# The last 16 channels of a four-layer transformer's LayerNorm: scaled and shifted on GpSimd before the transpose, rounded and split on VectorE after it

## The chip, the cores and the metric

The program runs on one core of a Trainium2 chip. The metric is the device time of one execution in microseconds. The kernel before took 1564.3 us (median of 3 runs, 1563.18 to 1565.5).

## The reference

Four transformer layers run over 32 sequences of 128 tokens with 144 channels, in fp32. Each layer reads a condition vector and makes six rows per sequence from it: shift, scale and gate for attention, and the same for the MLP. What a layer does (layer 0; its MLP is a mixture of four experts, of which two are used per token):

```
mod = silu(c) @ w_adaln + b_adaln
sh_msa, sc_msa, g_msa, sh_mlp, sc_mlp, g_mlp = split(mod, 6)
h = layernorm(x) * (1 + sc_msa) + sh_msa
q, k, v = h @ w_qkv + b_qkv            # 16 heads of 9 channels
x = x + g_msa * (softmax(q k^T / 3) v @ w_proj + b_proj)
h = layernorm(x) * (1 + sc_mlp) + sh_mlp
x = x + g_mlp * mlp(h)                 # 144 -> 576 -> 144, gelu
```

Layers 1 to 3 have a plain MLP. Layer 2 uses an RMS norm in place of the LayerNorm, norms q and k by head, and passes its gates through tanh.

## The kernel before

**Blocks.** The 32 sequences are taken four at a time: a layer's attention has eight groups, its MLP eight steps. Each norm of four sequences is a block with a number k (16 per layer: eight for attention, eight for the MLP), 64 in all. `ORDER` lists the order in which the blocks are made and `NTH[k]` is a block's place in it.

**One block's norm.** The statistics come from VectorE (`stats`, L1443 and L1448), the factor from GpSimd (`factor`), and the normed rows `xn` (token by channel) from GpSimd (`rows`, L1923 and L1925) or in the MLP steps from VectorE (`normalise`). TensorE multiplies by channel, so `xn` is turned: its first 128 channels by `t_main` (L574), and ScalarE scales and shifts them by channel while it takes them out of PSUM (`mod_main`, L1166). The last 16 channels go a way of their own. GpSimd's `copies` (L1934) writes them four times side by side into `xr`, `t_rem` (L581) turns the 64 columns into 64 rows of a PSUM bank, and VectorE's `mod_rem` (L1471) scales and shifts them by channel into `hmod`, in four instructions, one for each sequence. ScalarE's `round_rem` (L1177) rounds `hmod` to `hhi` (fp32r), and VectorE's `split_rem` (L1477) writes `hr`, where two of the four copies carry the rounded value and two what it lacks. `hr` and `hT` are then the operands of every product of the block.

**The scales and shifts** for these 16 channels lie in `modr`, turned (channel by sequence). At the start, for each layer, TensorE computes `mod` (`layer_mods`), VectorE takes it out of PSUM (`mods_out`, L1847 and L1848), TensorE turns it (`turn_mods`) and VectorE takes it out again (`take_mods`, L1855 and L1856).

**Attention.** A group has eight units u, each for two head groups. In one unit TensorE makes scores for the maxima five units ahead (L648), VectorE takes the maxima (`head_max`, L1534), TensorE turns them (`turn_max`, L655, which waits for `d_on`), makes the scores again with the maxima taken off (L666, L670), ScalarE takes the exponential (L1223), TensorE weighs the values (L682) and turns the result (L690), and VectorE divides (`normed`, L1552, tile `On`). All engines run through lists written out by hand, in program order, and wait for semaphores alone. At u = 0 TensorE runs `t_rem` of the block three groups on, VectorE `mod_rem`; at u = 1 ScalarE rounds and VectorE splits, and TensorE waits for `d_hm` before it uses bank 5 again; at u = 4 and 5 VectorE takes the statistics of the next block, and GpSimd then makes its factor, its rows and its copies, in this order and after its other work of the group (`copy_rest`, `parts23`, `add_to_x`).

**DMAs.** q and k are written to DRAM and read back in another order (`write_parts`, L415 and L418, `read_parts`, L445, twelve DMAs for each block), all issued by SP in its own list. For each block SP also loads the gates, one row of DRAM to all 128 partitions (`load_gates`, L394). They were stored at the start by `save_gates` (L329). In the first group, SP's list is: write and read block 0's q and k, store the gates of the four layers, write and read block 1's, load the gates, load the rest of x and weights.

Of the kernel before, what the change touches and what calls it, by code (L numbers as in the profile page):

```python
# [7 lines left out]
F32 = mybir.dt.float32  # L8
# [11 lines left out]
L = 4  # L20
# [29 lines left out]
AHEAD = 5  # L50

# [47 lines left out]

def slot_of(k):  # L100
    l, which, g = k // 16, k % 16 // 8, k % 8
    if which == 0 and g < 3:
        return g if l == 0 else 2
    return g % 2


def build(nc, io):
    ctx = ExitStack()
    with ctx:
# [28 lines left out]
        modr = sb("modr", [REM - 2, L, 4, B])  # L138
# [7 lines left out]
        hmod = sb("hmod", [REM - 2, TG])  # L146
# [15 lines left out]
        ohi = hhi  # L162
# [30 lines left out]
        gsb = wfc2_f[0:2 * B, 0:L * C].rearrange("b (l n) -> b l n", l=L)  # L193
        vt = [wfc1[0:TOK_V[0], E - 1, 0:TG], wfc2[0:TOK_V[1], E - 1].rearrange("p k c -> p (k c)")[:, 0:TG]]
# [37 lines left out]
        cw_scr = nc.dram_tensor("cw_scr", [2, E, G, T], F32, kind="Internal").ap()  # L232
        gate_scr = nc.dram_tensor("gate_scr", [L, 2, B, C], F32, kind="Internal").ap()
# [31 lines left out]
        s_mod, d_ms = sem("s_mod"), sem("d_ms")  # L265

# [23 lines left out]
        def normal(k):  # L290

            return (d_xn, CR + 4 * (NTH_DVE[k] + 1)) if k in NTH_DVE else (g_xn, CR + 4 * (NTH_POOL[k] + 1))

# [14 lines left out]
        def _(sp):  # L308
# [157 lines left out]
            def attention(l):  # L466
                n0, m0 = 8 * l, 16 * l
                if l == 0:
                    write_parts(0, 0)
                    read_parts(0, 0)  # L470
                    for i in range(L):
                        save_gates(i)
                    write_parts(0, 1)
                    read_parts(0, 1)
                    sp.wait_ge(q_gs[0], 16)
# [4 lines left out]
                    for i in range(1, L):  # L480
                        sp.wait_ge(q_gs[i], 16)
                if l == 2:
                    write_parts(l, n0 + 1)
                    read_parts(l, n0 + 1)
                for g in range(8):
# [5 lines left out]
                    load_gates(m0 + g + 1)  # L491
                    if l == 0:
# [13 lines left out]
            def mlp(l):  # L506
# [8 lines left out]
                for g in range(8):  # L515
                    if g < 7 or l < 3:
                        load_gates(m0 + g + 1)
                    if l == 0 and g in (1, 2, 3):
# [23 lines left out]
        def _(pe):  # L542
# [16 lines left out]
            def turn_mods(l):  # L559
# [3 lines left out]
                for s in range(2):  # L563
                    pe.transpose(bank[4][:, 2 * B * s:2 * B * s + 2 * B], mods_m[:, s, :], ident[0:2 * B, 0:2 * B])
                for s in range(2):
# [181 lines left out]
            def attention(l):  # L747
# [39 lines left out]
                else:  # L787
                    pe.wait_ge(d_hm, CR + 4 * (NTH[m0 + 2] + 1))
                start_layer(l)
                for g in range(8):  # L790
                    n, m = n0 + g, m0 + g
                    new = turned_at(l, g)
                    for u in range(UNITS):
# [34 lines left out]
                        if u == 1 and g > 0:  # L828
                            if new is not None:
                                pe.wait_ge(d_hm, CR + 4 * (NTH[new] + 1))  # L830
# [32 lines left out]
                        elif u == 6 and g < 6:  # L863
# [4 lines left out]
                            else:  # L868
                                pe.wait_ge(d_hm, CR + 4 * (NTH[new] + 1))
                            values(l, n + 2, 1, 5)  # L870

            def values_unit(g, u, n, m, new):

                if u == 5 and g < 7:
# [4 lines left out]
                    else:  # L879
                        pe.wait_ge(d_hm, CR + 4 * (NTH[new] + 1))  # L880
# [8 lines left out]
            def by_token_unit(g, u, n, m, new):  # L889
# [16 lines left out]
                if u == 5 and g < 5:  # L906
                    if g:
                        pe.wait_ge(d_gate, CR + 2 * m)
                    else:
                        pe.wait_ge(d_hm, CR + 4 * (NTH[new] + 1))  # L910
# [14 lines left out]
            def mlp(l):  # L925
# [72 lines left out]
                def before(g):  # L998
# [4 lines left out]
                    if l < 3 and g in (4, 6):  # L1003
# [3 lines left out]
                        return (a_ht, CR + 4 * (NTH[k] + 1)), (d_hm, CR + 4 * (NTH[k] + 1))  # L1007
# [9 lines left out]
                    return (a_ht, CR + 4 * (NTH[m - 1] + 1) if m - 1 >= m0 else 0), (d_hm, CR + 4 * (NTH[m - 1] + 1))  # L1017

                def after_tile(g, t):
# [30 lines left out]
                    if l == 1 and g == 6 and t == 1:  # L1050
                        pe.wait_ge(d_hm, CR + 4 * (NTH[M + 1] + 1))
# [7 lines left out]
                def after_seq(g, b):  # L1059

                    first_of = turned_mlp(l, g)[0] if turned_mlp(l, g) else None
                    if l < 3 and g in (3, 5) and b == 1:
                        i = NTH[first_of]
                        turn(M + (g - 3) // 2, (a_ht, CR + 4 * (i + 1)), (d_hm, CR + 4 * (i + 1)))
                    if l == 1 and g in (4, 6):
                        n = N + (g - 4) // 2
                        o = 7 - b % 2
                        if b == 0:
                            pe.wait_ge(d_hm, CR + 4 * (NTH[first_of] + 1))
# [16 lines left out]
                    if l in (0, 2) and g in (4, 6) and b > 0:  # L1086
                        n = N + (g - 4) // 2
                        if b == 1:
                            pe.wait_ge(d_hm, CR + 4 * (NTH[first_of] + 1))
# [45 lines left out]
                if l == 1:  # L1135
                    pe.wait_ge(d_hm, CR + 4 * (NTH[M + 2] + 1))
# [17 lines left out]
        def _(act):  # L1154
# [15 lines left out]
            outs, rounds = [], []  # L1170

            def round_rem(k):
                act.wait_ge(d_hm, CR + 4 * (NTH[k] + 1))
                act.wait_ge(d_hr, CR + NTH[k])
                act.wait_ge(d_onr, CR + len(outs))
                rounds.append(k)
# [57 lines left out]
            def out_rem(n, o):  # L1234
                act.wait_ge(s_onr, CR + n + 1)
                act.wait_ge(d_onr, CR + n)
                act.wait_ge(d_hr, CR + len(rounds))
                outs.append(n)
                act.activation(ohi[:], bank[o][0:REM - 2, :], ACT.Copy).then_inc(a_oa, 1)

            def attention(l):
# [24 lines left out]
                for g in range(8):  # L1266
# [3 lines left out]
                    for u in range(UNITS):  # L1270
# [7 lines left out]
                        if u == 1 and new is not None:  # L1278
# [841 lines left out]
```

## Time and profile before

| | before |
|---|---|
| median of 3 runs | 1564.3 us |
| span of the profiled execution | 1547.8 us |
| TensorE busy | 1415.6 us, 91% |
| VectorE busy | 1036.5 us, 67% |
| ScalarE busy | 778.5 us, 50% |
| GpSimd busy | 542.2 us, 35% |
| mean granted TensorE clock | 0.969 |

The page gives the profiled execution's span, from its first to its last instruction, and no time of its own beside it. The median of the runs is 16.5 us above that span. Engines are named PE (TensorE), DVE (VectorE), ACT (ScalarE), POOL (GpSimd), SP; a busy share is an average over stages with different limits. An idle time in brackets behind an instruction names what ended it.

### The profile page before, as it was taken

What the parts mean: (1) busy time and instruction counts of PE and PEld (TensorE: products, weight loads), DVE (VectorE), ACT (ScalarE), POOL (GpSimd) and SP (SyncE); (2) the same over time, 40 slices, a digit from 0 to 9 for tenths busy, and PEclk for the clock granted to TensorE, in tenths of its full rate; (3) what the DMA queues carried; (4) which work ended last, traced back from release to release, by engine and by line L of the source; (5) the groups of instructions that cost most, each with busy time, mean ns of one, the idle gap of its engine ahead of it and who ended that gap; (6) DMA issues with size and microseconds to landing.
All of it is one profiled execution on the core that took longest, in us unless ns stands there. A gap on an engine that the chain in (4) does not pass through costs nothing. (4 is left out here: it accounts for less than half of the span.)

```text
span 1547.8 us, 41007 instructions
## 1 busy us (share of the span) xinstructions
PE 1415.6 (91%) x15976; PEld 1065.0 (69%) x15976; DVE 1036.5 (67%) x2592; ACT 778.5 (50%) x1287; POOL 542.2 (35%) x739
## 2 busy tenths in 40 slices
PE   5799988999999998999899778877999799999998
PEld 2377776777777776777676656766777577767776
DVE  4688885766676667888537689887446466666342
ACT  2377763333333335767645456665544266555543
POOL 3355532211131313555323423443335244343322
PEclk9799999999999999999999889999999899999999
DMA  4765631111122032565000333443116667775021
GB/s 129 149 163 147 161 88 52 51 44 44 35 58 75 19 94 62 144 150 138 20 31 22 104 95 104 109 115 104 33 36 86 114 102 109 138 138 97 24 55 47
DMA packets 209128, 134.92 MB, mean 87 GB/s; under 512 B 142461, under 2 KB 191320, under 8 KB 202730
## 3 DMA queue, kind: packets, MB, share of 16 engines
q1 hardware_dynamic: 188978, 129.74, 35.4%
q10 hardware_dynamic: 19960, 2.57, 1.2%
q8 instruction: 129, 2.11, 0.6%
q14 instruction: 61, 0.50, 0.1%
HBM read 98.24 MB, written 33.24 MB: 85 GB/s over the span
## 5 line engine op out<-in xcount | busy, mean ns | idle before, releaser
L1534 DVE TENSOR_REDUCE negm<-banks 128x8 bf16<-128x1024 f32 x256 | 311.1, 1215 | 79.0 <-PE banks L648 77.2
L1223 ACT ACTIVATE prob<-banks 128x1024 f32<-128x1024 f32 x256 | 262.3, 1025 | 194.0 <-PE banks L670 193.3
L1351 ACT ACTIVATE hid<-banks 128x512 f32<-128x512 f32 x144 | 85.9, 597 | 230.5 <-PE banks L951 230.5
L1954 POOL TENSOR_TENSOR X<-X,gx 128x288 f32<-128x288 f32 x128 | 104.7, 831 | 256.9 <-DVE gx L1564 255.1
L967 PEld LDWEIGHTS banks<-wfc,hid 128*128 128x128 f32 x1152 | 157.0, 190 | 30.0 <-issue 19.9
L666 PE MATMUL banks<-qk 54*128 54x128 bf16 (+1 forms) x2048 | 169.4, 236 | 5.7 <-ACT prob L1223 5.0
L670 PE MATMUL banks<-mT,identb 64*128 64x128 bf16 x2048 | 166.2, 225 | 0.3 <-issue 0.3
L967 PE MATMUL banks<-wfc,hid 128*128 128x144 f32 x1152 | 161.4, 286 | 0.0
L648 PE MATMUL banks<-qk 54*128 54x128 bf16 (+1 forms) x2048 | 123.3, 242 | 39.8 <-DVE negm L1534 24.9
L950 PE MATMUL banks<-hT,wfc 128*128 128x512 f32 x288 | 149.1, 599 | 1.7 <-DMA wfc<-in_L_cond_w 1.2
L1725 DVE TENSOR_TENSOR hid<-hid,qk 128x512 f32<-128x512 f32 x128 | 88.9, 695 | 88.8 <-ACT hid L1351 80.4
L682 PE MATMUL banks<-prob,V 128*32 128x128 f32 x4096 | 142.8, 281 | 0.0
L1471 DVE TENSOR_SCALAR hmod<-banks,modr 64x128 f32<-64x128 f32 x256 | 86.8, 396 | 77.4 <-PE banks L581 77.0
L1939 POOL CAST parts<-res 96x512 bf16<-96x512 f32 x96 | 58.5, 609 | 220.9 <-DVE res L1484 220.0
L1376 ACT ACTIVATE hid<-banks 128x512 f32<-128x512 f32 (+1 forms) x120 | 71.0, 595 | 122.1 <-PE banks L941 121.1
L987 PE MATMUL banks<-wfc,hid 128*128 128x144 f32 (+1 forms) x960 | 128.0, 290 | 0.2 <-DVE gx L1564 0.2
L648 PEld LDWEIGHTS banks<-qk 54*128 54x128 bf16 (+1 forms) x2048 | 70.2, 102 | 82.0 <-DVE negm L1534 38.1
L987 PEld LDWEIGHTS banks<-wfc,hid 128*128 128x128 f32 (+1 forms) x960 | 123.9, 194 | 3.9 <-issue 2.7
L940 PE MATMUL banks<-hT,wfc 128*128 128x512 f32 x240 | 123.5, 595 | 0.0
L682 PEld LDWEIGHTS banks<-prob,V 128*32 128x32 f32 x4096 | 106.7, 112 | 16.8 <-issue 6.4
L666 PEld LDWEIGHTS banks<-qk 54*128 54x128 bf16 (+1 forms) x2048 | 109.2, 101 | 9.6 <-ACT prob L1223 7.3
L1166 ACT ACTIVATE hT<-banks,modm 128x128 f32<-128x128 f32 x256 | 98.8, 453 | 33.2 <-PE banks L574 33.1
(165 smaller groups left out, 2799.2 us busy)
## 6 DMA issues: line engine op xcount, KB each, us to landing
qk<-qk_scr SPq DMA_DIRECT2D x96, 216.0 KB
gbuf<-gate_scr SPq DMA_DIRECT2D x64, 288.0 KB, 4.3
qk_scr<-parts SPq DMA_DIRECT2D x48, 288.0 KB, 2.7
qk<-qk_scr SPq DMA_DIRECT2D x96, 144.0 KB
qk<-cw_scr SPq DMA_DIRECT2D x8, 1024.0 KB, 4.7
qk_scr<-parts SPq DMA_DIRECT2D x48, 144.0 KB, 2.5
qk<-qk_scr SPq DMA_DIRECT2D x96, 72.0 KB
qk<-tok_scr SPq DMA_DIRECT2D x32, 216.0 KB
```

Source lines behind the costliest of these rows:

```text
L648: mm = pe.matmul(bank[s][:, T * i:T * i + T], operand(l, 0, n, U, s, i), operand(l, 1, n, U, s, i), start=True, stop=True)
L666: pe.matmul(bank[2 + s][:, at], operand(l, 1, n, U, s, i), operand(l, 0, n, U, s, i), start=True, stop=False)
L670: mm = pe.matmul(bank[2 + s][:, at], one_hot(half, 64 * s + 4 * (u % 2) + i, [64, T]), mT[half, u // 2, :], start=False, stop=True)
L682: mm = pe.matmul(bank[4][32 * i:32 * i + 32, T * (2 * s + u % 2):T * (2 * s + u % 2 + 1)], V[:, n % 3, u // 2, VS * h:VS * h + 32], prob[: ...
L940: pe.matmul(bank[2 + i % 2][:], wfc1_t[:, at:at + 128], hT[:, h, :], start=True, stop=False)
L950: pe.matmul(bank[2 + i % 2][:], w, hT[:, h, :], start=True, stop=False)
L967: mm = pe.matmul(bank[4 + b // 2][:, C * (b % 2):C * (b % 2) + C], hid[:, i % KT, T * b:T * b + T], wfc2[:, e - (t == KT - 1), t, :], star ...
L987: mm = pe.matmul(bank[4 + q][:, C * (b % 2):C * (b % 2) + C], hid[0:rows, t, T * b:T * b + T], wfc2[0:rows, k, t, :], start=(t == 0), stop ...
L1166: act.activation(hT[:, slot_of(k), T * b:T * b + T], bank[o][:, T * b:T * b + T], ACT.Identity, scale=modm[:, l, 2 * w + 1, at:at + 1], bi ...
L1223: act.activation(prob[:, 2 * (U % 3):2 * (U % 3) + 2, :], pairs[1][:], ACT.Exp, scale=scale).then_inc(a_exp, 1)
L1534: dve.tensor_reduce(negm[:, u // 2, :, 4 * (u % 2):4 * (u % 2) + 4], pairs[0][:].rearrange("q s (h k) -> q s h k", k=T), AX.X, ALU.max, ne ...
L1954: pool.tensor_tensor(x, x, gx[:, q, :, :], ALU.add).then_inc(g_x, 1)
```

## The change

The last 16 channels are scaled and shifted by token, before they are turned. The condition rows of these channels (shift, and one plus scale) are written by VectorE to `msr` and stored by SP to a new DRAM tensor `mod_scr`, one store for each layer (`save_mods`), each right behind that layer's gate store. For each block from the fourth on (`FIRST = 3`), SP loads the block's rows, 128 numbers, to all 128 partitions, into one of four buffers `mrow` (`load_mods`). GpSimd's `copies` multiplies the 16 channels in place and adds the shift while it writes them four times. After the transpose VectorE rounds (`tensor_copy`) and splits in two instructions that both read the PSUM bank (`round_and_split`), both at the place of `mod_rem`; `split_rem` at unit 1 and ScalarE's `round_rem` are gone. TensorE's waits for `d_hm` become waits for `d_hr` (`rem_taken`). The first three blocks keep the old way. `modr` holds layer 0 alone; for the other layers the transposes of its rows and their copies are left out. `hmod` and `modr` lie in other tiles' room, and `ohi` has room of its own, so ScalarE's `out_rem` no longer waits for the split of a norm.

```diff
+            def save_mods(l):
+                sp.wait_ge(d_ms, CR + l + 1)
+                sp.dma_start(mod_scr[l].rearrange("w b s c -> (w b) s c"), msr[:, l]).then_inc(q_ms[l], 16)
+
+            def load_mods(k):
+                i, l, w, g = NTH[k], k // 16, k % 16 // 8, k % 8
+                sp.wait_ge(q_ms[l], 16)
+                if i >= FIRST + NMR:
+                    sp.wait_ge(g_xr, CR + i - NMR + 1)
+                sp.dma_start(mrow[:, i % NMR].rearrange("t b s c -> t (b s c)"),
+                             mod_scr[l, w, G * g:G * g + G].rearrange("b s c -> (b s c)").unsqueeze(0)
+                             .to_broadcast([T, G * 2 * CR_CH])).then_inc(q_mr[i % NMR], 16)
...
                     for i in range(L):
                         save_gates(i)
+                        save_mods(i)
                     write_parts(0, 1)
                     read_parts(0, 1)
+                    load_mods(3)
+                    for k in prepared_in(0, 0, 0):
+                        load_mods(k)
                     sp.wait_ge(q_gs[0], 16)
                     load_gates(0)
...
                     load_gates(m0 + g + 1)
+                    for k in prepared_next(l, 0, g):
+                        load_mods(k)
...
+            def round_and_split(k, o):
+                dve.wait_ge(s_hr, CR + NTH[k] + 1)
+                dve.wait_ge(d_hr, CR + NTH[k])
+                dve.tensor_copy(hhi[:], bank[o][0:REM - 2, :]).then_inc(d_hi, 1)
+                dve.wait_ge(d_hi, CR + NTH[k] - FIRST + 1)
+                dve.scalar_tensor_tensor(hr[0:REM - 2, slot_of(k), :], hhi[:].bitcast(F32), masks[0:REM - 2, 0:1],
+                                         bank[o][0:REM - 2, :], ALU.mult, ALU.add).then_inc(d_hr, 1)
...
                         if u == 0 and new is not None:
-                            mod_rem(new, 5)
-                        if u == 1 and new is not None:
-                            split_rem(new)
+                            round_and_split(new, 5)
...
-                pool.tensor_copy(xr[:, p], xn[:, p, :, CM:C].unsqueeze(2).to_broadcast([T, G, 4, CR_CH])).then_inc(g_xr, 1)
+                if k < FIRST:
+                    pool.tensor_copy(xr[:, p], xn[:, p, :, CM:C].unsqueeze(2).to_broadcast([T, G, 4, CR_CH])) \
+                        .then_inc(g_xr, 1)
+                    return
+                pool.wait_ge(q_mr[i % NMR], 16 * ((i - FIRST) // NMR + 1))
+                x, by = xn[:, p, :, CM:C], mrow[:, i % NMR]
+                pool.tensor_tensor(x, x, by[:, :, 1, :], ALU.mult).then_inc(g_ml, 1)
+                pool.wait_ge(g_ml, CR + i - FIRST + 1)
+                pool.tensor_tensor(xr[:, p], x.unsqueeze(2).to_broadcast([T, G, 4, CR_CH]),
+                                   by[:, :, 0, :].unsqueeze(2).to_broadcast([T, G, 4, CR_CH]), ALU.add).then_inc(g_xr, 1)
```

## Rows read from the trace of the kernel before

**Rows 1.** The page's busy times: us, share of the span, instructions.

```profile
PE 1415.6 (91%) x15976; PEld 1065.0 (69%) x15976; DVE 1036.5 (67%) x2592; ACT 778.5 (50%) x1287; POOL 542.2 (35%) x739
```

**Rows 2.** TensorE's waits: line, releaser: us in total, times, longest.

```profile
PE banks L655 <- DVE On L1552: 33.2, 42, 1.6
...
PE banks L648 <- DMA qk<-qk_scr: 9.9, 7, 2.8
PE banks L581 <- POOL xr L1934: 8.3, 12, 1.8
```

**Rows 3.** Stretches: length; PE, PEld, DVE, ACT, POOL busy (count); clock; DMA share; GB/s.

```profile
65.00:242.00 177.00, 164.55 (x2973) 126.48 (x2977) 147.99 (x332) 120.97 (x174) 88.00 (x110) 0.97 0.55 136
...
900.00:1108.00 208.00, 170.45 (x3048) 137.60 (x3050) 175.25 (x419) 130.99 (x214) 80.78 (x131) 0.96 0.36 94
```

**Rows 4.** Tiles `hmod`, `hhi`: ns min/median/max; one wait: us, times.

```profile
L1471 DVE TENSOR_SCALAR hmod<-banks,modr x256: 390/394/404, 19.5 to 1529.2; 64x128 f32<-64x128 f32 x128
...
L1477 DVE SCALAR_TENSOR_TENSOR hr<-hhi,masks,hmod x64: 739/744/1225, 22.4 to 1530.3; 64x512 fp32r<-64x512 f32 x64
  ACT hhi L1177: 43.7, 59
...
L1558 DVE SCALAR_TENSOR_TENSOR onr<-hhi,masks,banks x32: 728/734/742, 97.8 to 1460.5; 64x512 fp32r<-64x512 f32 x32
```

**Rows 5.** GpSimd by line: ns min/median/max, first and last start.

```profile
L1934 POOL COPY xr<-xn x39: 396/396/852, 89.1 to 1094.4; 128x256 f32<-128x256 f32 x39
...
L1903 POOL TENSOR_TENSOR rstd<-mv x16: 195/198/214, 800.0 to 1187.3; 128x4 f32<-128x4 f32 x16
...
L1954 POOL TENSOR_TENSOR X<-X,gx x128: 779/795/1259, 102.2 to 1544.1; 128x288 f32<-128x288 f32 x128
```

**Rows 6.** Order of time, layer 0, groups 3, 4: start, us, what, [idle before].

```profile
148.49 1.22 DVE L1534 TENSOR_REDUCE negm<-banks 128x8 bf16<-128x1024 f32 x1 [0.32 <-PE banks L648]
...
158.50 0.40 POOL L1934 COPY xr<-xn 128x256 f32<-128x256 f32 x1
...
159.04 0.60 PE L581 MATMUL banks<-ident,xr 128*64 128x128 f32 x4 [0.26 <-POOL xr L1934]
```

**Rows 7.** Order of time: the first and the last of 17 hand-overs.

```profile
89.14 0.41 POOL L1934 COPY xr<-xn 128x256 f32<-128x256 f32 x1
...
89.70 0.38 PE L581 MATMUL banks<-ident,xr 128*64 128x128 f32 x2
...
1068.43 0.40 POOL L1934 COPY xr<-xn 128x256 f32<-128x256 f32 x1
...
1068.97 0.49 PE L581 MATMUL banks<-ident,xr 128*64 128x128 f32 x3 [1.36 <-POOL xr L1934]
```

**Rows 8.** Order of time, TensorE, layer 2, group 3, unit 3.

```profile
992.96 0.23 PE L655 MATMUL banks<-identb,negm 128*128 128x128 bf16 x1 [1.59 <-DVE On L1552]
...
994.17 0.40 PE L648 MATMUL banks<-qk 54*128 54x128 bf16 x8 [0.98 <-DMA qk<-qk_scr]
```

**Rows 9.** The start: SP's reads; DMA landings of L394 (all; 59:61), L329; TensorE; clock.

```profile
55.69 4.24 SPq L445 DMA_DIRECT2D qk<-qk_scr  x12
...
DMA to landing us min/median/max: 3.0/4.3/14.1
...
DMA to landing us min/median/max: 14.1/14.1/14.1
...
DMA to landing us min/median/max: 1.8/7.9/10.1
...
66.98 1.06 PE L581 MATMUL banks<-ident,xr 128*64 128x128 f32 x4
...
54.00:67.00 13.00, 6.05 (x83) 3.87 (x83) 7.61 (x8) 2.31 (x2) 3.40 (x5) 0.50 0.69 134
```

**Rows 10.** Layer 3: SP's waits from 1325 to 1395 us; TensorE at 1390.

```profile
SPq L450 <- DMA v_scr<-wfc: 18.1, 3, 6.9
...
1390.94 0.64 PE L648 MATMUL banks<-qk 62*128 62x128 bf16 x8 [2.16 <-DMA qk<-tok_scr]
```

More of the change, by code:

```diff
@@ L50 @@
 AHEAD = 5
+FIRST = 3
+NMR = 4
 def norm_order():
@@ L97, with prepared_in, prepared_next @@
 NTH_DVE = {k: i for i, k in enumerate(BY_DVE)}
+def prepared_in(l, w, g):
+    if w:
+        return prepared_mlp(l, g)
+    return [turned_at(l, g + 1)] if g < 6 else [16 * l + 8 + g - 4]
+def prepared_next(l, w, g):
+    l, w, g = l + (w and g == 7), (w + (g == 7)) % 2, (g + 1) % 8
+    return prepared_in(l, w, g) if l < L else []
 def slot_of(k):
@@ L137, in build @@
         modm = sb("modm", [CM, L, 4, B])
-        modr = sb("modr", [REM - 2, L, 4, B])
+        mrow = sb("mrow", [T, NMR, G, 2, CR_CH])
         gbuf = sb("gbuf", [T, 2, G, C])
@@ L232, in build @@
         cw_scr = nc.dram_tensor("cw_scr", [2, E, G, T], F32, kind="Internal").ap()
+        mod_scr = nc.dram_tensor("mod_scr", [L, 2, B, 2, CR_CH], F32, kind="Internal").ap()
         gate_scr = nc.dram_tensor("gate_scr", [L, 2, B, C], F32, kind="Internal").ap()
@@ L265, in build @@
         s_mod, d_ms = sem("s_mod"), sem("d_ms")
+        q_ms, q_mr = [sem(f"q_ms{l}") for l in range(L)], [sem(f"q_mr{i}") for i in range(NMR)]
+        g_ml, d_hi = sem("g_ml"), sem("d_hi")
         block = ctx.enter_context(nc.Block())
@@ L517, in mlp @@
                         load_gates(m0 + g + 1)
+                    for k in prepared_next(l, 1, g):
+                        load_mods(k)
                     if l == 0 and g in (1, 2, 3):
@@ L563, in turn_mods @@
                 for s in range(2):
-                    pe.transpose(bank[4][:, 2 * B * s:2 * B * s + 2 * B], mods_m[:, s, :], ident[0:2 * B, 0:2 * B])
-                for s in range(2):
+                    mm = pe.transpose(bank[4][:, 2 * B * s:2 * B * s + 2 * B], mods_m[:, s, :], ident[0:2 * B, 0:2 * B])
+                for s in range(2 if l == 0 else 0):
                     mm = pe.transpose(bank[4][0:REM - 2, 2 * B * (s + 2):2 * B * (s + 3)],
@@ L829, in attention @@
                             if new is not None:
-                                pe.wait_ge(d_hm, CR + 4 * (NTH[new] + 1))
+                                pe.wait_ge(*rem_taken(new))
                             else:
@@ L868, in attention @@
                             else:
-                                pe.wait_ge(d_hm, CR + 4 * (NTH[new] + 1))
+                                pe.wait_ge(*rem_taken(new))
                             values(l, n + 2, 1, 5)
@@ L879, in values_unit @@
                     else:
-                        pe.wait_ge(d_hm, CR + 4 * (NTH[new] + 1))
+                        pe.wait_ge(*rem_taken(new))
                     values(3, n + 1, 1, 5)
@@ L909, in by_token_unit @@
                     else:
-                        pe.wait_ge(d_hm, CR + 4 * (NTH[new] + 1))
+                        pe.wait_ge(*rem_taken(new))
                     q_and_k_by_token(n + 3, 0, 5)
@@ L1847, in mods_out @@
                 dve.tensor_copy(mods_m, src[:, :, 0:CM])
-                dve.tensor_copy(mods_r, src[:, :, CM:C].unsqueeze(2).to_broadcast([2 * B, 2, 4, CR_CH])).then_inc(d_ms, 1)
+                if l == 0:
+                    dve.tensor_copy(mods_r, src[:, :, CM:C].unsqueeze(2).to_broadcast([2 * B, 2, 4, CR_CH]))
+                dve.tensor_copy(msr[:, l, 0], src[:, 0, CM:C])
+                dve.tensor_scalar(msr[:, l, 1], src[:, 1, CM:C], 1.0, None, ALU.add).then_inc(d_ms, 1)
             def take_mods(l):
                 dve.wait_ge(s_mod, CR + l + 1)
-                for out, src in ((modm[:, l], bank[4][:, 0:4 * B]), (modr[:, l], bank[4][0:REM - 2, 4 * B:8 * B])):
+                both = ((modm[:, l], bank[4][:, 0:4 * B]), (modr[:], bank[4][0:REM - 2, 4 * B:8 * B]))
+                for out, src in both if l == 0 else both[:1]:
                     out = out.rearrange("c (w s) b -> c w s b", s=2)
```

48 lines of the change are left out of this document (20 added, 28 removed).

## The prediction

> **What bounds the kernel now.** I read the page first, then TensorE's waits, the busy times by stage, the tiles that the change touches, and last the order of time around each hand-over. TensorE is busy 91% of the span and VectorE 67% [rows 1]. What frees VectorE is therefore worth something only where TensorE waits for it. The list of TensorE's waits is short: 33.2 us for `On` ahead of the transpose of the maxima (L655), and 8.3 us in 12 waits for GpSimd's `xr` (L581) [rows 2]. The `On` waits lie mostly in layer 2's attention: there VectorE is busy 175.25 of 208 us and TensorE 170.45, while in layer 0's attention TensorE has 164.55 of 177 us [rows 3]. So VectorE is near its limit in one stage of four, and the path that starts each group's LayerNorm transpose (statistics on VectorE, then GpSimd, then L581) is tight elsewhere.
>
> **What the change removes.** For 61 of the 64 blocks, VectorE's four scale-and-shift instructions go (394 ns each by the median), and ScalarE's rounding, for which VectorE stood idle 43.7 us in 59 waits before its split (744 ns) [rows 4]. What comes in their place is one copy out of PSUM and one split that reads PSUM. The split has a twin: the attention output's one, 734 ns [rows 4]. The copy (64x512 to SBUF) has no row of its own shape; it lies between one of the 394 ns pieces (a quarter of it) and the 734 ns of the two-operand form. I take 0.65 us. So at unit 0 of a group VectorE does 0.65 + 0.05 for its own semaphore + 0.73 = 1.4 us, where it did 4 x 394 = 1.6 us with overlaps (1.36 from first to last), and in unit 1 some 0.65 us of split and up to 0.6 us of waiting go. VectorE gains about 1.3 us a group, TensorE sees bank 5 released at the same time within 0.1 us. ScalarE's 61 roundings are off the path: none of TensorE's listed waits names them; I cost them at nothing.
>
> **What it is worth in layers 0, 1 and 3: nothing.** In layer 0's group 3 (groups and units count from 0), before the statistics that start GpSimd, VectorE already stands idle for TensorE's scores (0.32 us at 148.49) [rows 6]. A VectorE that reaches that point earlier waits longer, and the statistics at unit 5 come when they came.
>
> **What it is worth in layer 2's attention.** There TensorE waits 1.59 us for `On` at unit 3, and right behind that 0.98 us for a q/k read [rows 8]. With the split gone from unit 1, `On` is 0.66 us earlier (0.744 less the overlap). In the groups where the q/k read lands last (of TensorE's seven such waits, 9.9 us in all [rows 2], one each in groups 2, 3, 4 and 6) this is handed to the DMA. Groups 0, 1 and 5 keep it: 3 x 0.66 = 2.0 us. Against it stand 0.3 us for the new semaphore step ahead of TensorE's unit 1. I take -1.7 (0 to -4: all six groups keep it).
>
> **What it adds on GpSimd.** `copies` was one COPY of 256 elements a partition, 396 ns. Now it is a product over 64 elements, a semaphore, and a sum over 256 written with repeats. GpSimd's two-operand rows are 198 ns at 4 elements and 795 ns at 288 [rows 5], so 2.1 ns an element: 0.20 + 60 x 2.1 ns = 0.33, and 0.20 + 252 x 2.1 ns = 0.72. With 0.08 between (the spacing of dependent steps of GpSimd) that is 1.13, less 0.40: **0.73 us more**. Ends: 0.28 (the sum as cheap as the copy, the product at the 198 ns floor) and 1.3 (both at the 0.795 of 288 elements).
> Is it hidden? At 158.50 GpSimd starts the copy, 0.40 us, and L581 starts at 159.04, 0.14 us after its end, having waited 0.26 us [rows 6]. The same 0.14 to 0.15 us separates the two in 17 attention groups (six of layer 0, six of layer 1, five of layer 2; the first and the last in [rows 7]) and in two steps of layer 1's MLP. In these the copy's end is what releases TensorE or comes with it, so each lengthens by 0.73, unless another wait follows that was already longer:
> - layer 0: five groups pay, the sixth loses it to a 1.6 us wait for q/k, another of the seven: 5 x 0.73 = 3.65;
> - layer 1: five pay and the sixth in part (0.3): 3.95;
> - layer 1's MLP: 2 x 0.73 = 1.5;
> - layer 2: covered by the `On` wait at unit 1 and the q/k waits: 0. If that cover goes, 3.6.
> In layer 3 the copy stands over 4 us ahead of its reader: 0.
>
> **What it adds on SP's queue, at the start.** Block 3's copies now wait for `mrow`, whose load SP issues behind the twelve q/k reads of the second block. Those reads start at 55.69 and take SP 4.24 us; the gate load issued right behind them, at 60.03, lands 14.1 us later, at 74.1, where the median of its kind takes 4.3 us [rows 9]. The load of block 3 takes its place ahead of the gates. Lower end: the small gate stores issued behind the first block's reads waited up to 10.1 us [rows 9], which is 14.3 us after that block's first read (35.4), so 55.9 + 14.3 = 70.2 here (the four new stores cost SP about one issue, 0.4 us, the shorter set-up gives back 0.2). Upper end: 74.3. I take the middle, 72.3. Then 1.13 for the pair and 0.15 to TensorE: L581 at 73.6 instead of 66.98 [rows 9], **+6.6** (4.5 to 8.6). GpSimd's copy was done at 57.5 before, so this cover of 9.5 us is eaten whole. TensorE stands idle meanwhile behind L581, with q/k of block 2 and the next scores queued after it. The 0.7 us wait for a q/k read in group 1, the shortest but one of the seven, goes: -0.7. The clock: from 54 to 67 us it was granted 0.50, the lower level of 1.2 GHz, with TensorE busy 6.05 of 13 us [rows 9]; after a longer idle time work that ran at 2.4 GHz will run at the lower level a while: +1.0 (0 to 3). Sum of the start: **+6.9**.
> The set-up also loses two small transposes and two small VectorE instructions for each of three layers, about 0.5 us, which now only lengthens the wait.
>
> **What it adds on SP's queue later.** One more issue for each block (0.34 us, as the gate load) and 64 KB in 512-byte rows. In layers 0 to 2 it follows the group's reads, and the next writes are far off: 0. In layer 3 SP is itself late: between 1325 and 1395 us it waits for no `parts` at all, only for `v_scr` (18.1 us in 3 waits) and its own writes, and TensorE waits 2.16 us for q/k at 1390.94 [rows 10]. Each turn of that loop gets 0.4 us of issue and up to as much of transfer; four turns before the wait at 1390.94, at 0.5 each: **+2.0** (0 to 4).
>
> **Sum**: start 6.9, layer 0 3.65, layer 1 3.95, its MLP 1.5, layer 2 -1.7, layer 3 2.0: +16.3. The profiled execution's span is 1547.8 us and becomes 1564.1. The median of the runs, 1564.3, is 16.5 us above that span; I carry this over unchanged: 1564.3 + 16.3 = **1580.6 us**, 1.0% slower.
>
> **The rivals.**
> 1. *The load overtakes the reads.* If `mrow` lands some 3 us after its issue at 60.4, block 3 is ready at 64.7, ahead of 66.98, and the start costs 0 in place of 6.9: 1573.7. For it: the four `gate_scr` stores had a minimum of 1.8 us; against it: that one was issued after the reads were through, and the gate load took 14.1 us. 12%.
> The Trainium skill, "DMA: Bandwidth & Descriptors", section "Queues, rings and completion order", says that completion is not in order of issue, since one DMA may use fewer of the 16 engines than another; by it a small load on free engines could overtake. The gate load of the same 128-row form did not [rows 9].
> 2. *GpSimd's pair is cheap* (0.28 us): the 12.4 paying hand-overs cost 3.5 and not 9.1: 1575. 14%.
> 3. *Faster: VectorE's queue is the bound of the attention groups of layers 0 to 2.* It is busy 148 of 177 and 175 of 208 us [rows 3]. If each of 18 groups became shorter by the 1.3 us that VectorE saves, and GpSimd's delay went under it, -23.4 + 6.9 = -16.5: 1548. It decides from the point where the statistics of unit 5 come earlier than before. Against it: VectorE's idle time for scores just ahead of them [rows 6] and `xr` as TensorE's own wait. 9%.
> 4. *Heavier*: the pair costs 1.3 us, layer 2's cover gives way, and layer 3's loop takes 1 us a turn: 16.3 + 12.4 x 0.57 + 3 + 2 = +28.4: 1592.7. 12%.
> 5. A mixture near zero (rivals 1 and 2 together with all of layer 2's gain): 6.9 + 5.6 + 2.3 = 14.8 less of 16.3, so 1566: 5%.
> The forecast keeps 48%. Range for 8 in 10: 1568 to 1590, which leaves out rivals 3 to 5 for the most part. A measurement of this kernel tells about 0.2%, 3 us, from no change: slower 0.86, same 0.05, faster 0.09.
>
> **What would show it.** In the changed kernel's trace: L581 of block 3 (about 67 us before) starts at 72 to 75 us behind a wait of 5 us or more for GpSimd; GpSimd's pair takes 1.0 to 1.3 us; the waits of L581 for `xr` rise from 8.3 to some 22 us; layer 3's waits for `tok_scr` reads rise from 2.8 to near 5 us; VectorE's busy time falls by 50 us or more without shortening layers 0 and 1. I am wrong if layer 0's or layer 1's groups become shorter, or if block 3 starts on time.

## The result, and the profile after

The changed kernel takes 1581.43 us (median of 4 runs, 1572.6 to 1584.25); the kernel before took 1563.74 us beside it (4 runs, 1560.69 to 1565.5). The ratio is 1.0096 with a 95% interval of [1.0062, 1.013]: slower by 15 us (the two medians are 17.7 us apart). The forecast was 1580.6 us. The total is right, and the experiments below show that one of its terms was well off. Ratios, here and below, leave out runs more than 1.5% above the fastest of their kernel: 3 of 93 of the kernel before, and 2 of one other kernel.

The page of the changed kernel, its span and busy times (as [rows 1]):

```profile
span 1570.8 us, 40884 instructions
...
PE 1423.7 (91%) x15970; PEld 1072.7 (68%) x15970; DVE 1001.3 (64%) x2408; ACT 748.5 (48%) x1226; POOL 582.7 (37%) x800
```

VectorE lost 35 us of work, ScalarE 30, and GpSimd got 40.5 more. For VectorE 50 or more were predicted. That comes out (55) with the four scale-and-shift instructions at their full length of 394 ns each; they overlap, and with the 1.36 us from first to last that the prediction names itself it is 42. In layer 0's group 3 VectorE's busy time fell by 0.73 us (20.94 to 20.21, rows under the experiments), which makes 44 us for 61 blocks; the rest of the difference to 35 was not looked into. TensorE's waits in the changed kernel (as [rows 2]: line, releaser, us in total, times, longest; L627 is the old L581, L694 the old L648, L701 the old L655):

```profile
PE banks L627 <- POOL xr L1984: 26.5, 20, 6.9
...
PE banks L701 <- DVE On L1595: 23.9, 39, 1.8
PE banks L694 <- DMA qk<-qk_scr: 9.3, 6, 3.5
PE banks L694 <- DMA qk<-tok_scr: 9.1, 5, 2.9
```

Waits for `xr` rose from 8.3 to 26.5 us (predicted: some 22), those for `On` fell from 33.2 to 23.9.

**The start**, in order of time: SP's issue of block 3's load, GpSimd's pair, TensorE's transpose (as [rows 9]):

```profile
59.98 0.82 SPq L364 DMA_DIRECT2D mrow<-mod_scr  x2
...
73.52 0.32 POOL L1982 TENSOR_TENSOR xn<-xn,mrow 128x64 f32<-128x64 f32 x1 [15.76 <-DMA mrow<-mod_scr]
73.92 0.72 POOL L1984 TENSOR_TENSOR xr<-xn,mrow 128x256 f32<-128x256 f32 x1
...
74.70 0.64 PE L627 MATMUL banks<-ident,xr 128*64 128x128 f32 x2 [6.89 <-POOL xr L1984]
```

The load lands 13.4 us after its issue, at 73.4 (predicted 72.3), and L627 starts at 74.70 (predicted 73.6) behind 6.89 us of idle time. The landing, from the answer for that line:

```profile
DMA to landing us min/median/max: 13.4/13.4/13.4
```

The stretches around it (columns as in [rows 3]):

```profile
54.00:67.00 13.00, 5.53 (x74) 3.32 (x75) 7.60 (x8) 2.72 (x3) 3.65 (x5) 0.50 0.76 165
67.00:74.00 7.00, 0.80 (x16) 0.54 (x12) 0.00 (x0) 1.02 (x1) 0.40 (x2) 0.50 1.00 155
74.00:90.00 16.00, 14.20 (x192) 8.91 (x194) 9.71 (x17) 8.38 (x13) 5.93 (x7) 0.82 0.36 109
```

TensorE is idle for 6.2 of the 7 us from 67, and in the 16 us behind them the clock is granted at 0.82, a mixture of its two levels. Before, the transpose ran at 66.98 [rows 9]. Group 0 of layer 0 as a whole (from its first exponential to the next group's), before and changed:

```profile
64.93:87.23 22.30, 20.09 (x329) 14.11 (x333) 15.92 (x36) 14.55 (x22) 8.24 (x11) 0.87 0.74 158
```

```profile
65.69:95.52 29.83, 20.74 (x329) 14.57 (x333) 15.27 (x33) 14.04 (x20) 9.28 (x13) 0.76 0.56 123
```

It grew by 7.5 us, 6.9 of them the wait.

**The pair** on GpSimd in all 61 blocks (ns min/median/max, first and last start), and VectorE's two instructions:

```profile
L1982 POOL TENSOR_TENSOR xn<-xn,mrow x61: 317/319/382, 73.5 to 1534.0; 128x64 f32<-128x64 f32 x61
L1984 POOL TENSOR_TENSOR xr<-xn,mrow x61: 718/723/1121, 73.9 to 1534.4; 128x256 f32<-128x256 f32 x61
```

```profile
L1518 DVE CAST hhi<-banks x61: 673/682/684, 75.8 to 1551.3; 64x512 fp32r<-64x512 f32 x61
L1520 DVE SCALAR_TENSOR_TENSOR hr<-hhi,masks,banks x61: 737/740/740, 76.5 to 1552.0; 64x512 fp32r<-64x512 f32 x61
```

0.32 and 0.72 us stand against a predicted 0.33 and 0.72; 0.68 and 0.74 against 0.65 and 0.73.

**A hand-over of layer 0** (as [rows 6]), and the next one:

```profile
169.56 0.72 POOL L1984 TENSOR_TENSOR xr<-xn,mrow 128x256 f32<-128x256 f32 x1
...
170.42 0.38 PE L627 MATMUL banks<-ident,xr 128*64 128x128 f32 x2 [0.99 <-POOL xr L1984]
...
193.70 0.38 PE L627 MATMUL banks<-ident,xr 128*64 128x128 f32 x2 [1.00 <-POOL xr L1984]
```

The idle time was 0.26 us [rows 6] and is 0.99 now. From this hand-over to the next it is 193.70 - 170.42 = 23.28 us; before, the next one came at 181.58, 22.54 us on. That is 0.74 more in this group, as forecast (0.73):

```profile
181.58 0.60 PE L581 MATMUL banks<-ident,xr 128*64 128x128 f32 x4 [0.26 <-POOL xr L1934]
```

By stage, without the start: layer 0's groups 1 to 5 went from 114.2 to 118.1 us (+3.9, predicted 3.65), layer 1's attention from 171.9 to 175.1 (+3.2, predicted 3.95), its MLP from 135.8 to 138.8 (+3.0, predicted 1.5), layer 2's attention from 207.7 to 209.2 (+1.5, predicted -1.7), layer 3's from 218.8 to 224.4 (+5.6, predicted 2). Two traces can't settle such totals, and that the first two are near the forecast is in part luck. Layer 0's five groups changed by 0.0, +1.6, +0.7, +0.7 and +0.7 us: in group 1 the pair's 0.7 stands against a read wait of 0.65 us that did not come back, in group 2 another 0.9 us is not the pair's. In layer 1 the groups 3 and 4, for which 0.73 each were forecast, changed by 0.0 and +0.1, and group 5 grew by 1.7, of which 1.25 are an idle time of TensorE with no releaser in the profile. In the last three stages the changed kernel's trace has more time at the clock's lower level (3.7 us more in layer 1's MLP, 10 in layer 2's attention, 5.3 in layer 3's; 3.2 in layer 1's attention too), and such time comes and goes between executions of one kernel, as the next section shows.

### The profile page after: what moved, and what is told of

The parts are those of the page before. It is cut to its first block and busy times, and to the rows that moved or that the text cites. A ratio compares the mean times of both kernels' runs of the same rounds, so it can differ in the third digit from the quotient of the medians.

```text
span 1570.8 us, 40884 instructions
## 1 busy us (share of the span) xinstructions
PE 1423.7 (91%) x15970; PEld 1072.7 (68%) x15970; DVE 1001.3 (64%) x2408; ACT 748.5 (48%) x1226; POOL 582.7 (37%) x800
## 5 line engine op out<-in xcount | busy, mean ns | idle before, releaser
L694 PE MATMUL banks<-qk 54*128 54x128 bf16 (+1 forms) x2048 | 123.4, 242 | 46.0 <-DVE negm L1577 24.2
L728 PE MATMUL banks<-prob,V 128*32 128x128 f32 x4096 | 147.4, 287 | 0.0
L694 PEld LDWEIGHTS banks<-qk 54*128 54x128 bf16 (+1 forms) x2048 | 70.2, 102 | 89.0 <-issue 42.3
L728 PEld LDWEIGHTS banks<-prob,V 128*32 128x32 f32 x4096 | 109.9, 114 | 17.7 <-issue 7.2
L1992 POOL TENSOR_TENSOR parts<-res,parts 96x512 bf16<-96x512 f32 x96 | 112.7, 1174 | 7.7
```

What stands on the lines that cost most here:

```text
L694: mm = pe.matmul(bank[s][:, T * i:T * i + T], operand(l, 0, n, U, s, i), operand(l, 1, n, U, s, i), start=True, stop=True)
L728: mm = pe.matmul(bank[4][32 * i:32 * i + 32, T * (2 * s + u % 2):T * (2 * s + u % 2 + 1)], V[:, n % 3, u // 2, VS * h:VS * h + 32], prob[: ...
L1992: pool.tensor_tensor(parts[:, m, 2, :], res[:, i % 2, :], parts[:, m, 1, :], ALU.subtract).then_inc(g_p3, 1)
```

## What one trace can and can't tell here

The kernel before was profiled a second time, unchanged, in one run. What was on record:

> The kernel before, profiled once more, to see what of its first profile repeats. Theory (the first profile, 1547.8 us, was an execution with little time at the lower clock): span near 1560 us, time at the lower clock near 120 us in place of 94; the busy and idle pattern of layers 0 to 2 the same to 0.1 us outside stretches at the lower clock; tok_scr waits in layer 3 anywhere from 2 to 9 us. Rival (the profile is typical and the timed runs carry 16.5 us outside the span): span within 3 us of 1547.8.

Measured: 1572.84 us. Spans and mean granted clocks of the first and the second trace of the same kernel:

```profile
core 0: 1547.8 us, clock 0.969
```

```profile
core 0: 1571.0 us, clock 0.957
```

The second is 23.2 us longer. Its waits for `On` and `xr` are the same as in [rows 2]. Its waits for reads are longer: 12.0 us for `qk_scr` where the first had 9.9, and 6.0 us in 3 waits for `tok_scr` in layer 3 where the first had 2.8. So what I had expected of layers 0 to 2, the same pattern to 0.1 us, holds for the engines' own waits and not for the reads (layer 0's group 1 waits 1.41 us for one, 0.65 in the first trace):

```profile
PE banks L655 <- DVE On L1552: 33.1, 42, 1.6
PE banks L648 <- DMA qk<-qk_scr: 12.0, 8, 3.1
...
PE banks L648 <- DMA qk<-tok_scr: 6.0, 3, 3.0
```

Most of what grew is the same work in stretches at the lower level. Layer 1's group 4, first trace and second (columns as in [rows 3]):

```profile
681.88:704.89 23.01, 21.95 (x393) 16.70 (x396) 19.79 (x42) 16.25 (x24) 12.50 (x17) 1.00 0.61 152
```

```profile
692.40:719.16 26.76, 23.51 (x393) 17.80 (x395) 19.77 (x42) 16.27 (x24) 12.48 (x17) 0.94 0.52 126
```

The same 393 matmuls take 23.01 and 26.76 us; the clock is the difference in the row (1.00 and 0.94), with 1.56 of the 3.75 us in TensorE's busy time. The other 2.2 us are idle time: TensorE's longest wait in this group is 2.56 us with no releaser in the profile (0.36 in the first trace). What it waited for is not shown. In the 93 runs of the kernel before that stand beside my experiments, the time reaches from 1551.6 to 1585.0 us and the mean granted clock from 0.971 to 0.952; time at the lower level (the granted clock is 1.00 or 0.50, so it is twice what the mean lacks of 1, times the span) reaches from 90 to 152 us, and it correlates with the time at 0.85.

This corrects one step of the forecast. The "16.5 us" between the span and the median are nothing that lies around a span: in every run on record, of every kernel here, time less span is 1.8 to 1.9 us. [Rows 1] come from an execution with little time at the lower level, faster than the median one. The prediction carried the 16.5 us over from before to after, which did no harm: it makes the forecast the median before plus 16.3.

## The experiments

Each ratio is against the kernel before, timed in between on the same chip, with its 95% interval. The first kernels build the change up from its parts.

**VectorE's half alone.** GpSimd copies as before, VectorE has the new two instructions, and there is no store, load or wait for them. The kernel leaves out the scale and shift of the 16 channels from the fourth block on. Against the changed kernel (`save_mods`, `load_mods` and SP's waits for `q_ms` are out at all their places):

```diff
-                        save_mods(i)
...
-                    load_mods(3)
-                    for k in prepared_in(0, 0, 0):
-                        load_mods(k)
...
-                pool.wait_ge(q_mr[i % NMR], 16 * ((i - FIRST) // NMR + 1))
-                x, by = xn[:, p, :, CM:C], mrow[:, i % NMR]
-                pool.tensor_tensor(x, x, by[:, :, 1, :], ALU.mult).then_inc(g_ml, 1)
-                pool.wait_ge(g_ml, CR + i - FIRST + 1)
-                pool.tensor_tensor(xr[:, p], x.unsqueeze(2).to_broadcast([T, G, 4, CR_CH]),
-                                   by[:, :, 0, :].unsqueeze(2).to_broadcast([T, G, 4, CR_CH]), ALU.add).then_inc(g_xr, 1)
+                pool.tensor_copy(xr[:, p], xn[:, p, :, CM:C].unsqueeze(2).to_broadcast([T, G, 4, CR_CH])).then_inc(g_xr, 1)
```

> The changed kernel with GpSimd's single COPY of 256 elements as before, without the stores and loads of the condition rows and without the wait for them. Left out of the computation: scale and shift of the last 16 channels from the fourth block on. What stays is VectorE's and ScalarE's half of the change. My theory (only layer 2's attention waits for VectorE): layer 0 and 1 groups last as before (22.2 to 23.4 us), layer 2's attention gains 1 to 4 us, the whole is 0 to 5 us faster than before: ratio to before 0.997 to 1.000. Rival (VectorE's queue bounds the attention groups of layers 0 to 2): 18 groups shorter by 1.3 us each, 23 us faster, ratio 0.985.

Measured: 1554.36 us, ratio 0.9931 [0.9903, 0.996]. TensorE's waits:

```profile
PE banks L692 <- DVE On L1586: 26.4, 41, 1.4
...
PE banks L685 <- DMA qk<-tok_scr: 7.7, 5, 4.0
```

The half that I had priced at -1.7 us (0 to -4) gives -10.8 by its ratio. Layer 3's reads are to be seen as well: 7.7 us of waits for `tok_scr` in a kernel that loads nothing new.

**The same once more**, on another chip, with no edit:

> VectorE's half alone once more, beside the two kernels with part of the loads on the same chip: ratio 0.993 as before if its gain of 10 us is real, where my prediction allowed 0 to 4. Left out: as above. If it comes out above 0.997, the gain was a draw of the clock and the prediction's small figure stands.

Measured: 1555.45 us, 0.9946 [0.9914, 0.9977]. The mean of the two is 0.9938, 9.6 us. The gain stands, though this interval reaches up to -3.6 us, just inside my 0 to -4.

**With the stores and loads, unread.** The first kernel plus SP's four stores and 61 loads, for which nobody waits; it leaves out the same scale and shift. Against the changed kernel only GpSimd's part of the diff above is left: the wait and the pair go, the copy comes.

> As the kernel with VectorE's half alone, plus the four stores and the 61 loads, which nothing waits for and nothing reads. Left out of the computation: the same scale and shift. My theory (SP's list and the DMAs cost time in layer 3's attention alone): layer 3's attention longer by 3 to 6 us than in the kernel without loads, with TensorE's waits for tok_scr reads rising from under 3 us to 7 to 10 us; layers 0 to 2 and the start within 1 us. Rival (layer 3's longer waits come from the later phase against the clock or from VectorE's half): no difference between the two kernels.

Measured: 1559.13 us, 0.9977 [0.9949, 1.0005]: 4.8 us over the kernel without them by the medians, 7 by the ratios.

**With the wait.** GpSimd waits for `mrow` ahead of its copy, and still only copies. Against the kernel with the unread loads:

```diff
+                pool.wait_ge(q_mr[i % NMR], 16 * ((i - FIRST) // NMR + 1))
```

> As the one before, with GpSimd's wait for the loads kept, and the single COPY in place of product and sum. Left out of the computation: the same scale and shift. My theory: the first group pays for the load of block 3 alone, 6 to 7 us more than without the wait (L581's counterpart starts at about 74 us behind a wait of 6 us), and nothing else moves. Against the changed kernel it shows the price of the pair: 0.65 us for each of some 12 to 13 hand-overs, so 8 to 10 us faster than the changed kernel. Rival (the pair is hidden but for the first group): within 2 us of the changed kernel.

Measured: 1565.55 us, 1.0007 [0.998, 1.0035]: +6.4 us by the medians, +4.7 by the ratios. The first copy behind the wait starts at 75.1 us, so it is this wait and no other (GpSimd stands idle for it for 16.2 us, once). In its trace group 0 of layer 0 takes 29.95 us, where the kernel without the wait has 21.74:

```profile
L1981 POOL COPY xr<-xn x61: 397/398/477, 75.1 to 1532.1; 128x256 f32<-128x256 f32 x61
```

**The loads ahead of the reads.** The complete change, but the loads of blocks 3 and 4 are issued between the writes and the reads of block 1's q and k:

```diff
                     write_parts(0, 1)
-                    read_parts(0, 1)
                     load_mods(3)
                     for k in prepared_in(0, 0, 0):
                         load_mods(k)
+                    read_parts(0, 1)
```

> The changed kernel, complete, with the loads for blocks 3 and 4 issued before the twelve q/k reads of block 1 in SP's list and not behind them. My theory (the load stands in the queue behind the reads): it lands within 3 to 4 us of its issue at 53 us, block 3's transpose starts at 66 to 68 us without a wait, and the kernel is 6 to 9 us faster than the changed one. Rival (the load is slow by itself, or the first group waits for something else next, as the clock): gain under 3 us.

Measured: 1568.75 us, 1.0025 [0.9996, 1.0053], 11 us less than the change by the ratios. The issue, and the landing of the first loads:

```profile
53.35 1.50 SPq L364 DMA_DIRECT2D mrow<-mod_scr  x2
```

```profile
DMA to landing us min/median/max: 4.1/4.3/4.4
```

GpSimd's sum is done at 59.45 us. TensorE's transpose waits for GpSimd no longer, and the clock rises in the stretch in which the changed kernel stood idle:

```profile
68.20 1.06 PE L627 MATMUL banks<-ident,xr 128*64 128x128 f32 x4
```

```profile
67.00:74.00 7.00, 6.76 (x83) 4.09 (x83) 3.46 (x5) 3.42 (x5) 1.27 (x2) 0.73 0.94 166
```

So the wait at the start has one cause, the load's place behind the twelve reads: the same load lands in 4.1 to 4.4 us ahead of them and in 13.4 us behind them. The Trainium skill, "DMA: Bandwidth & Descriptors", section "Why a DMA increments its semaphore by 16 and not by 1", says that a DMA runs on up to 16 engines that finish independently, and that only the full count means that all data landed. By that a load is as late as the latest of its parts. The landings of 13.4 and 4.3 us are in keeping with it; which engines held it back no run here shows.

This kernel is also the second way to the pair's price. It differs from the kernel with the unread loads by the pair, GpSimd's wait (which costs nothing here) and the order of the loads. It is 7.5 us slower by the ratios and 9.6 by the medians, on the same chip.

The next kernels start from this order and take the remaining costs one by one.

**Layer 3's loads earlier.** In layer 3's attention, the loads of groups 0 to 5 are issued ahead of `turn_values`:

```diff
                         if l == 3:
+                            for k in prepared_next(l, 0, g):
+                                load_mods(k)
                             turn_values(n0 + g + 2)
                     load_gates(m0 + g + 1)
-                    for k in prepared_next(l, 0, g):
+                    for k in prepared_next(l, 0, g) if l < 3 or g > 5 else []:
```

> The kernel with the early loads, and in layer 3's attention each block's load issued right behind the q/k reads, ahead of SP's wait for v_scr, and not between that wait and the next writes. Theory A (each load lengthens layer 3's loop of writes, reads and v_scr by its issue and its bytes): the issue leaves the loop, gain of 1 to 3 us over the kernel with the early loads, tok_scr waits near 4 us. Theory B (the tok_scr waits vary from run to run and do not come from the loads, since the kernel without any load had 7.7 us of them): no difference beyond 1 us.

Measured: 1564.05 us, 1.0008 [0.9986, 1.0029], which doesn't part from 1.0025. The wait that it was aimed at, for `tok_scr`, did not shrink: 9.0 us in 5 waits, where the kernel with the early loads has 6.6 in 3.

**The last 16 channels first.** GpSimd norms these channels of a block, makes the pair, and only then norms the first 128, in the attention blocks of layers 0, 1 and 3 (`part` is `rows` for a range of channels):

```diff
                 factor(k)
-                rows(k)
-                copies(k)
+                if k < FIRST or k // 16 == 2:
+                    rows(k)
+                    copies(k)
+                    return
+                part(k, slice(CM, C), g_xm)
+                copies(k, g_xm)
+                part(k, slice(0, CM), g_xn)
```

> The kernel with the early loads, and on GpSimd, in the attention of layers 0, 1 and 3, the last 16 channels normed first (4 x 64-partition-wide small instructions of 128x16), then the pair, and the 128 channels for the main transpose after it. Theory (GpSimd's chain from the statistics to xr releases TensorE in the groups of layers 0 and 1): xr is ready some 2.3 us earlier (3.4 us of rows become 1.1), TensorE's waits of L627 in layers 0 and 1 (0.6 to 1.8 us in each of 12 groups) go to zero, groups last 22.2 to 22.5 us, and the kernel is 8 to 14 us faster than the one with the early loads, 5 to 9 us faster than before. Rival (the groups are bound by something just behind, VectorE's On or the q/k reads): gain under 4 us.

Measured: 1560.03 us, 0.9965 [0.9943, 0.9988]. It beats both the change and, by 0.35%, the kernel before. GpSimd's order in one group, and TensorE's transpose, which starts without a wait:

```profile
153.79 2.16 POOL L1946 TENSOR_SCALAR xn<-X,mv,rstd 128x16 f32<-128x16 f32 x4
...
156.03 0.32 POOL L1999 TENSOR_TENSOR xn<-xn,mrow 128x64 f32<-128x64 f32 x1
156.43 0.73 POOL L2001 TENSOR_TENSOR xr<-xn,mrow 128x256 f32<-128x256 f32 x1
157.13 3.19 POOL L1946 TENSOR_SCALAR xn<-X,mv,rstd 128x128 f32<-128x128 f32 x4
...
157.64 0.60 PE L628 MATMUL banks<-ident,xr 128*64 128x128 f32 x4
```

Layer 0's group 3 took 23.44 us before and 24.18 in the changed kernel, and takes 22.76 here (group 4: 22.55, 23.27 and 22.13):

```profile
132.93:156.37 23.44, 21.75 (x393) 16.65 (x396) 20.94 (x44) 16.25 (x24) 13.51 (x17) 1.00 0.56 146
```

```profile
142.84:167.02 24.18, 21.75 (x393) 16.65 (x396) 20.21 (x41) 15.82 (x23) 14.09 (x18) 1.00 0.53 141
```

```profile
132.64:155.40 22.76, 21.82 (x393) 16.70 (x395) 20.06 (x41) 15.82 (x24) 15.77 (x22) 1.00 0.59 156
```

All three rows are at the clock's full level, so this comparison is clean of it.

**Both** (the two diffs together):

> Both of the above on top of the early loads. If the two are independent, the sum of their gains: 9 to 16 us faster than the kernel with the early loads.

Measured: 1559.14 us, 0.996 [0.9934, 0.9987]. Against the kernel with layer 3's loads earlier alone, beside it on the same chip, the order of the channels is worth 4.9 us by the medians, 7.5 by the ratios. Layer 3's edit again shows nothing of its own.

**Which loads cost.** VectorE's half again, with the loads of layers 0 to 2 alone and with layer 3's alone, unread:

```diff
             def load_mods(k):
+                if not (l < 3):      # the other kernel: l == 3
+                    return
```

> VectorE's half with the stores and the loads for the blocks of layers 0 to 2 alone (45 of 61; nothing waits for them). Left out of the computation: scale and shift of the last 16 channels from the fourth block on, as in VectorE's half. Theory A (the loads cost time only in layer 3's loop of writes and reads): as VectorE's half alone, ratio to before 0.992 to 0.995. Theory B (they cost where they delay q/k reads in layers 0 to 2 and the start): 3 to 7 us slower than VectorE's half.

Measured: 1560.96 us (1559.10 for the ten runs of the ratio), 0.9952 [0.9914, 0.9991].

> VectorE's half with the stores and the loads for layer 3's blocks alone (16 of 61). Left out: as above. Theory A: carries the whole cost of the loads, 3 to 7 us slower than VectorE's half alone. Theory B: as VectorE's half alone.

Measured: 1558.15 us, 0.9978 [0.9951, 1.0004], with 7.2 us of `tok_scr` waits in its trace. The kernel with no loads stood at 0.9946 beside them. The three intervals overlap, and the medians put the two kernels the other way round than the ratios do. Where the loads cost, and if layer 3 has a share in it, stays open.

## Why the prediction was right, and where it was not

The steps in the order of the build-up, by the ratios times 1564 us (the terms add up to the change by construction; each difference of two ratios is uncertain by 4 to 7 us):

| step | forecast, us | measured, us |
|---|---|---|
| VectorE's half, the copy and split and what goes from unit 1 | -1.7 | -9.6 (-10.8 and -8.4) |
| loads and stores, unread | +2.0 | +6.0 |
| GpSimd's wait at the start | +6.9 | +4.7 |
| the pair in place of the copy | +9.1 | +13.9 |
| sum | +16.3 | +15.0 |

(For the second row: 0.9977 less the mean of 0.9931 and 0.9946.)

The last steps can also be taken in the other order, over the kernel with the early loads: then the pair is 7.5 us and the start 11.1. The two steps together are the same 18.6 us, forecast 16.0.

- **The start: right**, in cause and size. The load did not overtake the reads (13.4 us); TensorE waited 6.89 us. Group 0 of layer 0 grew from 22.3 to 29.8 us, 7.5 where 7.6 was forecast for the wait and the clock. Moving the load removed the wait. Rival 1 is out.
- **The pair: right** in its price (0.32 + 0.08 + 0.72 us), and in what a hand-over pays (0.74). Rivals 2 and 4 (0.28 and 1.3 us) are out. The changed kernel against the one with the wait and the copy, groups 1 to 5 of layer 0: 118.1 and 114.5 us, +3.6 for a forecast of 3.65. In layer 1 groups 1 to 4 each grew by 0.7 and group 5 by 0.2 (its length taken from the kernel with layer 3's loads earlier, where the idle time of 1.25 us is absent): 3.0 for 3.95. The two hand-overs in its MLP wait 1.4 us for `xr` where they had not waited (forecast 1.5), and layer 2 pays 0.8 (below, forecast 0). That makes 8.8 us for a forecast of 9.1; 7.5 and 13.9 us are what the ratios make of the same step. Norming the 16 channels ahead of the rest took 5 to 9 us off (the same step with and without layer 3's edit). That is no second measurement of the pair, since it also takes away waits for `xr` that the kernel before had.
- **VectorE's half: mis-sized, the step that failed.** I gave layers 0, 1 and 3 nothing, since in one group VectorE stood idle ahead of its statistics [rows 6], layer 2 -1.7, and the MLP stages no term at all. Measured are -10.8 and -8.4. The idle gap was read rightly: the copy of `xr` ends at the same point of the group, to 0.03 us, in groups 1 to 6 of layer 0 with and without VectorE's half, and in most groups of layer 1. What I missed are the other places where VectorE releases TensorE. In layer 1's group 3 the block's rows are ready 0.76 us earlier: VectorE's statistics end 0.24 us earlier, and GpSimd's four norm instructions take 3.54 us where they took 4.06 (why is not shown). TensorE's transpose before and with VectorE's half:

```profile
662.01 0.27 PE L581 MATMUL banks<-ident,xr 128*64 128x128 f32 x1 [0.89 <-POOL xr L1934]
```

```profile
662.55 0.38 PE L618 MATMUL banks<-ident,xr 128*64 128x128 f32 x2
```

At the clock's full level the group takes 23.17 us before and 22.43 with VectorE's half (with the pair it is back at 23.15). In group 6 of layers 0 and 1 the waits for `On` are shorter by 0.8 and 0.9 us (1.10 to 0.34, 2.26 to 1.38). In layer 2's MLP the wait for the maxima (`negm`) fell from 5.4 us (5.3 in the second trace) to between 3.4 and 3.9 in all eleven kernels with VectorE's half, first row before, second with it:

```profile
PE banks L648 <- DVE negm L1534: 5.4, 2, 4.1
```

```profile
PE banks L685 <- DVE negm L1568: 3.8, 2, 2.5
```

These are some 4 us of waits, before what the reads take back. Rival 3 named VectorE's queue as a bound of the attention groups, but its sign (statistics earlier than before) shows in 3 of the 17 groups compared, by 0.1 to 0.2 us, and the pair's delay did not go under it. The rest of the 9.6 us I can't place. By the mean clocks the runs of VectorE's half have 114 and 116 us at the lower level and those of the kernel before 124 beside them; by the line through the 93 runs (0.43 us of time for each us at the lower level) this goes with 3 to 4 us. Why they have less was not tried.

- **Layer 2: the mechanism right.** TensorE's waits there before, with VectorE's half, and in the changed kernel:

```profile
PE banks L655 <- DVE On L1552: 21.6, 22, 1.6
PE banks L648 <- DMA qk<-qk_scr: 7.2, 4, 2.8
PE banks L581 <- POOL xr L1934: 3.5, 5, 1.4
```

```profile
PE banks L692 <- DVE On L1586: 17.0, 22, 1.4
PE banks L685 <- DMA qk<-qk_scr: 9.9, 6, 4.1
PE banks L618 <- POOL xr L1971: 3.5, 5, 1.4
```

```profile
PE banks L701 <- DVE On L1595: 14.1, 22, 1.7
PE banks L694 <- DMA qk<-qk_scr: 8.7, 5, 3.5
PE banks L627 <- POOL xr L1984: 7.2, 5, 2.1
```

VectorE's half takes 4.6 us off the waits for `On` (0.65 in each of groups 2 to 4, as forecast), and the reads take 2.7 back, in other traces of it up to 5.2: handed to the DMA, as I had said, and more of it than I had said. The pair then adds 3.7 us of waits for `xr` and takes 2.9 off those for `On`. So the cover held for most of it, 0.8 us aside.

- **Loads in layer 3: the size is inside the errors, its place was not shown.** The forecast named longer `tok_scr` waits as its sign, from 2.8 to near 5 us. They came (9.1), but they are 6.0 in the second trace of the kernel before and 7.7 in a kernel without any load. A sign that varies this much from run to run is none.
- **The total** hit in part by luck, because errors of opposite sign met: VectorE's half brought 7.9 us more than forecast, while the loads cost 4.0 more and start and pair together 2.6 more. The last two are within what the ratios can't tell. VectorE's half is not: neither of its two intervals holds -1.7 us.

## What to carry to other kernels

Work moved to an engine that releases TensorE costs its full difference at every hand-over for which TensorE waits last (here 0.73 us in layers 0 and 1, and next to nothing in layer 2, where another wait covers it). Look first whether the part that TensorE needs next can be made first on that engine, since that order alone turned +0.25% into -0.35% here. A load on which a critical step waits belongs ahead of a batch of reads in its issuer's list. Before you price a relief at nothing because of an idle gap, list every wait for the relieved engine in every stage, the quiet ones too: the gap can be real and the gain lie elsewhere. Before you read a difference of two single traces as the change's, put the granted clocks of the same stretch side by side.

## What I had not expected of the hardware

- Two executions of the kernel before differ by 23.2 us in span with a mean granted clock of 0.969 and 0.957, and over 93 runs by 33 us.
- In the group shown, GpSimd's norm of a 128x16 piece takes 2.16 us for four, 0.54 each, where 128x128 takes 3.19 for four, 0.80 each: an eighth of the elements for two thirds of the time. The fastest of all 200 such instructions took 0.42 us. By the slope of 2.1 ns an element I would have taken 0.2 us for a 128x16 piece.
- The same 64 KB load lands in 4.1 to 4.4 us ahead of the twelve reads and in 13.4 us behind them.
